# Two of four rounding steps of an FFN's gate moved from ScalarE and VectorE to GpSimd

## The reference, cut to what matters

```
x    = act_qdq(layernorm(x))
up   = act_qdq(x @ w_up.T)
gate = act_qdq(x @ w_gate.T)
sig  = fixed_qdq_u16(sigmoid(gate))     # clip(round(s * 65536), 0, 65535) / 65536
gate = act_qdq(gate * sig)
o    = act_qdq(gate * up)
out  = o @ w_down.T
# act_qdq(x): scale = max(|x|) / 32767; clip(round(x / scale), -32768, 32767) * scale
```

## Time and profile before

| | us |
|---|---|
| median of 3 runs | 504.14 (503.83 to 504.67) |
| profiled execution | 504.35 |
| its span, first to last instruction | 502.4 |
| the gate pass ends, up stage begins on ScalarE | 293.72 |
| last product of the up stage begins | 365.67 |
| product stage ends (all-reduce for `o`) | 429.21 |

### The profile page before, as it was taken

The page is one execution under the profiler, slowest core; times in us unless marked ns, Lnnn a source line. Parts: engine busy times, 40 slices in busy tenths (PEclk is TensorE's granted clock), DMA queues, the critical chain, the costliest instruction groups (busy, mean ns, idle before and its releaser), DMA issues.

```text
span 502.4 us, 6899 instructions
## 1 busy us (share of the span) xinstructions
PE 461.5 (92%) x2506; PEld 303.5 (60%) x2506; DVE 357.1 (71%) x660; ACT 257.0 (51%) x308; POOL 42.8 (9%) x51
## 2 busy tenths in 40 slices
PE   4999999998999979989999999999859997499997
PEld 3787885987488548754444444443324443388886
DVE  6464583688257753778535469999989888899995
ACT  3795141634142200528243379999977767334430
POOL 1111111242013110300000000000100000000000
PEclk9999999998999998999999999999979999599999
DMA  8920000200020020020000000000000000233441
GB/s 249 336 73 1 0 2 12 72 1 1 0 85 0 1 83 2 0 85 0 0 0 0 0 0 0 0 1 0 1 0 0 0 0 1 84 106 129 144 146 63
DMA packets 20653, 21.09 MB, mean 42 GB/s; under 512 B 809, under 2 KB 20376, under 8 KB 20632
## 3 DMA queue, kind: packets, MB, share of 16 engines
q1 hardware_dynamic: 20612, 20.82, 13.0%
q10 hardware_dynamic: 20, 0.00, 0.0%
HBM read 12.43 MB, written 8.39 MB: 41 GB/s over the span
## 4 chain that ended last, share of the span: by engine, by line
PE 56%; issue 17%; DVE 14%; ACT 10%; POOL 1%; DMA 1%; ACTq 0%; POOLq 0%; DVEq 0%
PE ps L660 13%; PE ps L635 10%; PE ps L640 5%; PE ps L483 4%; PE ps L462 4%; PE ps L487 4%; PE ps L479 4%; ACT ag L815 3%; PE ps L525 3%; ACT hid L822 3%; PE ps L442 3%; DVE hid L1215 2%; ACT gq L810 2%; PE ps L428 1%; PE ps L451 1%
## 5 line engine op out<-in xcount | busy, mean ns | idle before, releaser
L635 PE MATMUL ps<-xh,wuh 128*128 128x512 f16 x192 | 73.5, 383 | 9.7 <-DVE gq L1240 7.8
L635 PE MATMUL ps<-xh,wul 128*128 128x512 f16 x192 | 73.3, 382 | 0.0
L640 PE MATMUL ps<-xl,wuh 128*128 128x512 f16 x192 | 57.6, 382 | 0.0
L660 PE MATMUL ps<-wdh,oh 128*128 128x256 f16 x192 | 44.9, 281 | 9.3 <-DVE oh L1277 9.3
L1187 DVE TENSOR_REDUCE cols<-hid x12 | 27.4, 2286 | 30.5 <-ACT hid L804 30.5
L660 PE MATMUL ps<-wdl,oh 128*128 128x256 f16 x192 | 44.8, 280 | 0.0
L869 ACT ACTIVATE oq<-hid,cols 128x1536 int16 (+1 forms) x16 | 25.1, 1575 | 37.3 <-DVE ol L1279 33.4
L635 PEld LDWEIGHTS ps<-xh,wuh 128*128 x192 | 18.9, 98 | 35.3 <-issue 10.9
L804 ACT ACTIVATE hid<-ps 128x2048 f32 x12 | 22.5, 1876 | 34.5 <-PE ps L640 34.5
L635 PE MATMUL ps<-xh,wgh 128*128 128x512 f16 x96 | 36.4, 379 | 0.7 <-DVE xh L1175 0.7
L635 PE MATMUL ps<-xh,wgl 128*128 128x512 f16 x96 | 36.4, 379 | 0.0
(11 more groups left out here) (179 smaller groups left out, 901.7 us busy)
## 6 DMA issues: line engine op xcount, KB each, us to landing
x_scratch<-xa SPq DMA_DIRECT2D x4, 1024.0 KB, 4.4
xo<-x_scratch SPq DMA_DIRECT2D x16, 256.0 KB, 2.8
out_dram<-xo SPq DMA_DIRECT2D x16, 256.0 KB, 2.2
xa<-in_x SPq DMA_DIRECT2D x3, 1024.0 KB, 11.8
xa<-in_x SPq DMA_DIRECT2D x4, 256.0 KB, 4.6
wv<-in_L_xattn_W_qv SPq DMA_DIRECT2D x1, 1024.0 KB, 8.2
wr<-in_L_ffn_w_gate SPq DMA_DIRECT2D x1, 768.0 KB, 10.2
wr<-in_L_ffn_w_up SPq DMA_DIRECT2D x1, 768.0 KB, 11.6
```

Of the source, the lines that this page charges most:

```text
L635: pe.matmul(ps[hf][:, q, :], w_[:, d, ds(k * P, P)], xh[:, d, n], start=d == 0 and w_ is wh, stop=False)
L640: mm = pe.matmul(ps[hf][:, q, :], wh[:, d, ds(k * P, P)], xl[:, d, n], start=False, stop=d == KD - 1)
L660: mm = pe.matmul(ps[par][:, t, 0:D], o_[:, par, k, q], w_[:, k, :], start=not low and k == 0 and w_ is wdh, stop=low and k == KF - 1)
```

## The change

Three things:

1. The rounding of the gate (`gq`) of odd units moves from ScalarE to GpSimd, but for unit 1, which ScalarE still does. GpSimd does that of block k+1 ahead of the sigmoid of block k.
2. The rounding of the sigmoid (`sq`) of even units moves from VectorE to GpSimd, into `sq[0]`. It waits for the sigmoid and for the product before.
3. Odd units use a second buffer `sq[1]`, in the space of the gate weights, which are no longer needed. VectorE's `gated` is now for odd units only, and waits for the product two units before.

ScalarE's loop over k is written out instead of looped on the engine. The all-reduces 2 to 4 stand behind all of GpSimd's new instructions.

```diff
-    sq = place(a, "sq", [P, HALF], U16)
+    sq = [place(a, "sq0", [P, HALF], U16), place(copy_of(r_wg), "sq1", [P, HALF], U16)]
...
-            for n in range(1, 5):
+            def over_all(n):
+
                 pool.wait_ge(loc_rdy, n)
                 pool.partition_all_reduce(c_all[:, n:n + 1], c_loc[:, n:n + 1], P, RMAX).then_inc(all_rdy, 1)
+
+            def gate_int(k):
+
+                pool.tensor_scalar(gq[:, k, HALF:TOK], hid[:, k, HALF:TOK], c_cg, 1.0, ALU.mult, ALU.mult).then_inc(gqp_rdy, 1)
+
+            def sigmoid_int(k):
+
+                pool.wait_ge(sig_rdy, 2 * k + 1)
+                ge(pool, p_rdy, 2 * k - 1)
+                pool.tensor_scalar(sq[0][:], hid[:, k, 0:HALF], 65536.0, 1.0, ALU.mult, ALU.mult).then_inc(sqp_rdy, 1)
+
+            over_all(1)
+            pool.wait_ge(scales, 2)
+            for k in range(KF):
+                if k + 1 < KF:
+                    gate_int(k + 1)
+                sigmoid_int(k)
+            for n in range(2, 5):
+                over_all(n)
...
             def gate_sigmoid(k, hf):
                 u = k * 2 + hf
-                act.wait_ge(gq_rdy, u + 1)
+                if hf == 0:
+                    act.wait_ge(gq_rdy, k + 1)
+                else:
+                    act.wait_ge(gqa_rdy if k == 0 else gqp_rdy, max(k, 1))
...
-            gate_int(0, 1)
+            act.activation(gq[:, 0, HALF:TOK], hid[:, 0, HALF:TOK], ACT.Copy, scale=c_cg).then_inc(gqa_rdy, 1)
             gate_sigmoid(0, 0)
             gate_abs(0, 1)
-            with act.Fori(1, KF) as k:
+            for k in range(1, KF):
                 gate_int(k, 0)
                 gate_sigmoid(k - 1, 1)
                 gate_abs(k, 0)
-                gate_int(k, 1)
                 gate_sigmoid(k, 0)
                 gate_abs(k, 1)
...
             def gated(u):
 
-                k, hf = u // 2, u % 2
+                k = u // 2
                 dve.wait_ge(sig_rdy, u + 1)
-                ge(dve, p_rdy, u)
-                dve.tensor_scalar(sq[:], hid[:, k, hf * HALF:(hf + 1) * HALF], 65536.0, None, ALU.mult).then_inc(sq_rdy, 1)
+                ge(dve, p_rdy, u - 1)
+                dve.tensor_scalar(sq[1][:], hid[:, k, HALF:TOK], 65536.0, None, ALU.mult).then_inc(sq_rdy, 1)
 
             def gated_max(u):
                 k, hf = u // 2, u % 2
-                dve.wait_ge(sq_rdy, u + 1)
+                if hf == 0:
+                    dve.wait_ge(sqp_rdy, k + 1)
+                else:
+                    dve.wait_ge(sq_rdy, k + 1)
...
             for u in range(NU):
-                gated(u)
+                if u % 2 == 1:
+                    gated(u)
```

More of the change, by code:

```diff
@@ L252, in build @@
         half_free = [sem("half0_free"), sem("half1_free")]
+        gqa_rdy, gqp_rdy, sqp_rdy = sem("gqa_rdy"), sem("gqp_rdy"), sem("sqp_rdy")
         gq_rdy, ag_rdy, sig_rdy, sq_rdy, p_rdy, pq_rdy, au_rdy, o_rdy = map(
@@ L1204, in gated @@
             def gated(u):
-                k, hf = u // 2, u % 2
+                k = u // 2
                 dve.wait_ge(sig_rdy, u + 1)
-                ge(dve, p_rdy, u)
-                dve.tensor_scalar(sq[:], hid[:, k, hf * HALF:(hf + 1) * HALF], 65536.0, None, ALU.mult).then_inc(sq_rdy, 1)
+                ge(dve, p_rdy, u - 1)
+                dve.tensor_scalar(sq[1][:], hid[:, k, HALF:TOK], 65536.0, None, ALU.mult).then_inc(sq_rdy, 1)
             def gated_max(u):
                 k, hf = u // 2, u % 2
-                dve.wait_ge(sq_rdy, u + 1)
+                if hf == 0:
+                    dve.wait_ge(sqp_rdy, k + 1)
+                else:
+                    dve.wait_ge(sq_rdy, k + 1)
                 dve.wait_ge(ag_rdy, u + 1)
-                dve.tensor_tensor_reduce(hid[:, k, hf * HALF:(hf + 1) * HALF], ag[:, hf, :], sq[:], 1.0, 0.0,
+                dve.tensor_tensor_reduce(hid[:, k, hf * HALF:(hf + 1) * HALF], ag[:, hf, :], sq[hf][:], 1.0, 0.0,
                                          ALU.mult, ALU.max, pmx[:, u:u + 1]).then_inc(p_rdy, 1)
```

## The result

The changed kernel takes 510.0 us (median of 4, 509.8 to 510.24), the kernel before 504.08 (503.83 to 504.67). The ratio is 1.0116, 95% interval 1.0098 to 1.0133: slower by 5.9 us. The forecast was slower by 2.4. The sign was right, the size was far too small, and most of the loss comes from something the prediction never mentions.

What follows compares the result with a forecast made beforehand. The prediction took a ScalarE-VectorE loop of 11.58 us per pair as the bound, replaced by 11.98 through GpSimd holding. Its terms summed to 9p + 38.84, 56.84 at p = 2.0: +2.4 us, 506.6 us, range 503.6 to 521.0.

Steps and rivals of the forecast that it cites:

- The loop of 11.58 us: Up stage, odd units: ScalarE's absolute value, rounding and sigmoid, then VectorE's cast, `up_max` and product take 11.58 us per pair.
- the three gains of 0: Steady part: dropping ScalarE's odd rounding, dropping VectorE's even cast and adding a second `sq` buffer each gain nothing.
- The length p: Time of one new GpSimd instruction of 2048 elements, bounded between 1.91 and 3.64 us and taken as 2.0.
- "two-input rate" rival: GpSimd's new instructions run near its two-input rate, 2.3 to 3.64 us each: 509.6 to 524.4 us; chance 0.25.
- Holding, both ways: Up stage: VectorE's two-input product and a GpSimd instruction reading SBUF exclude each other for a whole instruction; first issued wins.
- "not held" rival: GpSimd is not held by the odd product, or nothing is held; pairs stay at 11.58: 503.7 us; chance 0.11.
- The string: Each pair: after an odd product, two GpSimd instructions then the even product, 0.05+2p+2.30; with the rest, 11.98 us per pair.
- 1.5 us for the middle: Middle of the up stage: at 11.98 us per pair, the cast of unit 9 comes at 355.82 against 354.29.
- "quicker than 1.84" rival: GpSimd instructions of 1.2 to 1.8 us; ScalarE's loop covers the middle, only the end moves: 504.2 to 504.8; chance 0.12.
- The start: Start of the up stage: GpSimd's two instructions end at 305.45, before the first product's old start of 305.60.
- The end: Last up-stage products: the all-reduce stands behind GpSimd's last cast and product 10 behind both, 0.9 us late on top.
- p + 6.92: Time from product 9's end to the last product's end, 8.92 us against 8.05 before.

Runs made afterwards that it cites:

- place_only: last_cast_dve with GpSimd's gate rounding made to wait for VectorE's odd cast, so that it runs under `up_max`: 503.11 us, ratio 0.9986.
- swap_only: last_cast_dve with ScalarE doing the odd unit's sigmoid ahead of the next even rounding: 501.62 us, ratio 0.9946.
- last_cast_dve: The changed kernel, but VectorE again does the cast of unit 10's sigmoid: 503.2 us, ratio 0.999.
- tiny_late: The kernel before plus one 128x1 GpSimd multiplication, waiting for product 9 and standing before the up-scale all-reduce: 509.97 us, ratio 1.0135.
- gate_half_again: The changed kernel with an extra 128x1024 GpSimd multiplication ahead of each gate rounding, run a second time for a profile: 515.05 us, ratio 1.0217.

## Why the prediction was wrong, point by point

- **The loop of 11.58 us and the three gains of 0** held. The pair stayed at 11.58, and place_only shows the loop bounding it by itself.
- **The length p.** Taken 2.0; unheld rows show 1.96 for `gate_int` and 1.89 for the cast. Right, and the "two-input rate" rival (0.25) is out.
- **Holding, both ways.** Shown: 3.72 for the even product, 3.14 for a GpSimd cast under an odd one. The "not held" rival is out. The string was taken 0.5 too long, though: from the odd product's end (325.17) to the even product's end (331.02) it took 5.85 us, not 0.05+2p+2.30 = 6.35, because both instructions were shorter and the handovers overlap. With the 5.63 behind it that makes 11.48 instead of 11.98, just under the loop; swap_only, where the string alone bounds a pair, has 11.39. The forecast's 1.5 us for the middle became 0 by the clock of the trace: there it went as in the "quicker than 1.84" rival (0.12), though with p of 1.9 to 1.96.
- **The start.** "Nothing is late up to p = 2.07" was wrong: product 0 took 3.10 us, since the first `gate_int` began at 300.10, behind a load. Counted from the stage's first scale, which came 0.66 us earlier than before, the middle is 0.66 us late through this.
- **The end** is the step that failed. It set the all-reduce at its own 0.35 us and 0.10 of handover behind GpSimd's last cast. Between the two lie 5.82 us. With them, the term p + 6.92 becomes about 14.7; measured, from product 9's end to product 11's, 14.33 against 8.05. So of the 6.3 us at the end the load is 5.8, and about 0.5 is left for what the forecast counted there, 0.9. last_cast_dve takes the load off the path, and the last cast with it, and the loss is gone; tiny_late adds next to nothing but the load and has 5.1 us at this place.

In sum, against the kernel before: −0.66 us up to the stage's first scale, +0.66 in start and middle, +6.3 at the end, +0.4 in the product stage, −0.7 behind it, for 6.0 of span. The first, and the last two, are in stretches that the change leaves alone: the product stage takes 61.24 to 62.18 us and what follows it 72.5 to 73.8 in the profiles that have it unchanged. The forecast's 2.4 was 1.5 in the middle and 0.9 at the end. The 1.5 did not come, and of the 0.9 some 0.5 did. Without the load that would have been no clear change, so the right sign is luck. I looked in the trace of before for the price of GpSimd's instructions and for held ports. Its first all-reduce came 72 us behind elementwise work, and the other three behind an all-reduce, so it couldn't show the price of a switch; but the listing of the changed kernel shows the new ones.

## What to carry to other kernels

An engine that "does nothing" may still have a state. Before giving GpSimd elementwise work near an all-reduce, count how often it turns from one kind to the other, and keep 6 us free ahead of the all-reduce whose result someone waits for (here 7 to 8 passed ahead of the first elementwise instruction); ending the elementwise work one unit early was enough here. And where several chains have nearly the same length, measure the removal of each alone and of all together: here 2.2, 0.2 and 4.3 us.

## What the runs showed of the hardware

- GpSimd between an elementwise instruction and an all-reduce: 5.82 to 5.97 us in four profiles, whether the elementwise one was 128x2048 or 128x1, and hidden where the queue had the time; from the all-reduce to the first elementwise instruction, 7.0 to 7.8 us, in which the wait for the gate's scale is included (ScalarE, which waits for the same scale, starts 0.7 us after the all-reduce in the changed kernel).
- A one-input GpSimd multiplication of 2048 float32 into 16 bits: 1.89 (constant) and 1.96 us (scale from a column); of 1024, 1.12.
- VectorE's product and GpSimd's casts exclude each other, and the one that runs is not broken off. A product that waited for a running GpSimd instruction came ahead of GpSimd's next one (315.62 in gate_half_again); one that arrived 0.4 us after the next had started waited for it (327.29 in the changed kernel). But a GpSimd instruction that waited for a product let VectorE's cast pass too, where that followed the product at once (305.72 in gate_half_again, 5.06 us), and did not where it came 1.0 us later (316.26, 4.00 us).
